# The second narrow self attention of a decoder, kept in float32 row bands with its projections and its end inside one loop, in place of split bf16 stacks through HBM

## The reference

```python
def layer_norm(x, w, b, eps=1e-05): ...
def attention(x, w_qkv, b_qkv, w_o, b_o):          # H = 16, dh = 8, B = 4, T = 512
    qkv = x @ w_qkv + b_qkv
    q, k, v = jnp.split(qkv, 3, axis=-1)           # each (B, T, 16, 8)
    scores = jnp.einsum('bqhd,bkhd->bhqk', q, k) / jnp.sqrt(jnp.float32(dh))
    probs = jax.nn.softmax(scores, axis=-1)
    ctx = jnp.einsum('bhqk,bkhd->bqhd', probs, v).reshape(B, T, D)
    return ctx @ w_o + b_o
h = x + attention(layer_norm(x, ln1_w, ln1_b), w_qkv, b_qkv, w_o, b_o)
return h + moe_ff(layer_norm(h, ln2_w, ln2_b), w_gate, w1, b1, w2, b2)
```

## Time and profile before

| | us |
|---|---|
| median of 3 runs (lowest, highest) | 2156.8 (2144.95, 2158.94) |
| the profiled execution: its time, its span | 2162.13, 2160.4 |
| from the end of stage b's last `XT` copy (565.7) to the end of stage c's (970.9) | 405.2 |
| TensorE, VectorE, ScalarE busy over the span | 1709.4, 1297.4, 1013.1 |
| mean granted TensorE clock over the span | 0.893 |

### The profile page before, as it was taken

The page is one execution under the profiler, slowest core; times in us unless marked ns, Lnnn a source line. Parts: engine busy times, 40 slices in busy tenths (PEclk is TensorE's granted clock), DMA queues, the critical chain, the costliest instruction groups (busy, mean ns, idle before and its releaser), DMA issues. The chain is left out here.

```text
span 2160.4 us, 32545 instructions
## 1 busy us (share of the span) xinstructions
PE 1709.4 (79%) x9889; PEld 969.6 (45%) x9942; DVE 1297.4 (60%) x4106; ACT 1013.1 (47%) x1938; POOL 153.7 (7%) x280
## 2 busy tenths in 40 slices
PE   4187877287416955969999499999999989989997
PEld 2044444154201321336777344454545455656664
DVE  7388896565735844733333487767676745764445
ACT  3188884075103633643334167667576643332221
POOL 2000000300100000010000100000000002330000
PEclk8599998598756987988999799999999998998999
DMA  1533400340152124001000110000000000000000
GB/s 56 81 40 40 44 0 3 57 56 8 41 81 31 20 26 44 1 3 40 20 20 10 39 40 1 1 1 1 1 1 1 1 1 3 1 1 23 22 15 27
DMA packets 57630, 48.74 MB, mean 23 GB/s; under 512 B 12692, under 2 KB 53048, under 8 KB 57528
## 3 DMA queue, kind: packets, MB, share of 16 engines
q1 hardware_dynamic: 57527, 47.45, 13.8%
HBM read 38.30 MB, written 8.91 MB: 22 GB/s over the span
## 5 line engine op out<-in xcount | busy, mean ns | idle before, releaser
L557 DVE TENSOR_REDUCE c_NM<-ps_t 128x1 f32<-128x512 f32 x256 | 169.9, 688 | 96.9 <-PE ps_t L437 95.2
L1556 ACT ACTIVATE d_PT<-ps_t 128x512 f32<-128x512 f32 x256 | 150.5, 589 | 105.8 <-PE ps_t L1472 105.8
L1547 ACT ACTIVATE d_PR<-d_PR,d_NM 128x512 f32<-128x512 f32 x256 | 183.9, 718 | 32.9 <-DVE d_NM L1618 32.9
L437 PE MATMUL ps_t<-KX,QX 96*128 (+1 forms) x256 | 108.3, 428 | 105.6 <-DVE c_IB L575 46.8
L619 ACT ACTIVATE c_PT<-ps_s 128x1024 f32<-128x1024 f32 x128 | 130.4, 1024 | 126.6 <-PE ps_s L460 124.5
L2358 DVE SCALAR_TENSOR_TENSOR X<-ps_t,GATE,X 128x128 f32<-128x128 f32 x272 | 76.6, 344 | 185.3 <-PE ps_t L2283 185.3
L762 ACT ACTIVATE a_PR<-a_PR,a_NM 128x128 f32<-128x128 f32 (+3 forms) x256 | 129.8, 555 | 78.8 <-DVE a_NM L743 78.8
L1618 DVE CUSTOM_DVE_ANT_0 d_PR<-ps_s,d_BH 128x512 f32<-128x512 f32 x256 | 165.4, 683 | 0.3 <-PE ps_s L1463 0.2
L672 PE MATMUL ps_t<-ident,a_PR 128*128 128x128 f32 x640 | 117.9, 295 | 49.8 <-ACT a_PT L686 37.4
L2320 ACT ACTIVATE f_HT<-ps_s,f_BE 128x512 f32<-128x512 f32 x128 | 87.9, 687 | 128.6 <-PE ps_s L2273 127.8
L1463 PE MATMUL ps_s<-d_K,d_Q 64*128 64x512 f32 x512 | 145.0, 644 | 1.3 <-DVE d_NM L1618 1.3
(11 more groups left out here) (330 smaller groups left out, 2989.8 us busy)
## 6 DMA issues: line engine op xcount, KB each, us to landing
QX<-split_parts SPq DMA_DIRECT2D x108, 128.0 KB
KX<-split_parts SPq DMA_DIRECT2D x72, 128.0 KB
f_W<-in_L_ffn_w SPq DMA_DIRECT2D x16, 256.0 KB, 3.1
split_parts<-a_PARTS SPq DMA_DIRECT2D x8, 384.0 KB, 10.3
split_parts<-c_PARTS SPq DMA_DIRECT2D x8, 384.0 KB, 10.6
g_W<-in_L_ffn_w SPq DMA_DIRECT2D x24, 128.0 KB, 2.3
split_parts<-b_PARTS SPq DMA_DIRECT2D x4, 384.0 KB, 10.7
X<-in_x SPq DMA_DIRECT2D x4, 256.0 KB
```

The lines of the kernel that those rows point to most:

```text
L437: nc.tensor.matmul(c.ps_t[:, i % 2, :], QX[0:SROWS, bass.ds(head, 1), qt * P:(qt + 1) * P], KX[0:SROWS, bass.ds(head, 1), :], start=True, ...
L557: nc.vector.tensor_reduce(NM[:, qt, j:j + 1], c.ps_t[:, i % 2, :], AX.X, ALU.max, negate=True).then_inc(maxed, 1)
L1547: nc.scalar.activation(PR[:, n % RING, e, :], PR[:, n % RING, e, :], ACT.Exp, scale=-1.0, bias=NM[:, n % RING, e:e + 1], accum_out=DEN[:, ...
L1556: nc.scalar.activation(PT[:, g % 2, e, :, qt * P:(qt + 1) * P], c.ps_t[:, e, :].rearrange("p (k q) -> p k q", q=P), ACT.Copy).then_inc(tak ...
```

## The change

Stage c no longer uses the stacks, the split or HBM. Queries and keys are projected group by group inside the loop, with weights padded so that head `j` of a group lies at partitions 32j to 32j+7 of `QG` and `KG` (float32). `score` multiplies 8 rows in float32, in the row group of its head (array tiles of 32 rows x 128 columns); row 32j+8 of `KG` is one (a bias) and row 32j+8 of `QG` gets the negated maxima, so `score_by_key` multiplies 9 rows. The maxima are turned once in float32 (16 x 128) and written by four DMAs a step. The names: `MBANKS`, two banks for the tiles whose maxima are taken; `KPAIRS`, two pairs of banks for the exponents; `ps_f`, the one bank that projections, turned maxima, turned heads and the output projection share in a fixed order (`shared_bank_free`). `score` runs 24 tiles ahead of `score_by_key`. Value products are 512 columns an instruction. The output projection, residual, norm and `XT` copy of a batch are spread over the steps of the next one. All 16 steps are written out, with no hardware loop. The weights are loaded by `finish` of stage b, ahead of its own (`early`). Stage b's block no longer sets rows 96 to 127 of `KX` to one. With it the stores and loads of `split_parts` for stage c, 8 and 72 DMAs, are gone.

```diff
+class NarrowWeights:
+    def __init__(self, c, tag, ctx):
+        self.W = c.sb(f"{tag}_W", [P, 3, P], F32, ctx)
+        self.WO = c.sb(f"{tag}_Wo", [P, P], F32, ctx)
+        self.BROW = c.sb(f"{tag}_Brow", [1, 3, P], F32, ctx)
+        self.BV = c.sb(f"{tag}_Bv", [P, P], F32, ctx)
+        self.BO = c.sb(f"{tag}_Bo", [P, P], F32, ctx)
+        self.WB = c.sb(f"{tag}_WB", [P, 2], F32, ctx)
+        self.loaded = c.sem(f"{tag}_w")
...
+    MAXIMA_LEAD = 24
+    ALL = STEPS * TILES
+    MBANKS = [c.ps_s[:, i, :] for i in range(2)]
+    KPAIRS = [c.ps_s[:, 2:4, :], c.ps_t[:, :, :]]
+    PTS = 3
...
+        QG = c.sb(f"{tag}_QG", [P, 3, S], F32, own)
+        KG = c.sb(f"{tag}_KG", [P, 3, S], F32, own)
+        VG = c.sb(f"{tag}_VG", [P, 2, QT, H, CW], F32, own)
+        NM = c.sb(f"{tag}_NM", [P, 2, GH, QT], F32, own)
+        NMT = c.sb(f"{tag}_NMT", [TILES, 2, P], F32, own)
+        PT = c.sb(f"{tag}_PT", [P, PTS, GH, S], F32, own)
...
+        def head(j, rows):
+            return slice(CW * j, CW * j + rows)
...
+                for u in range(STEPS):
+                    sp.wait_ge(s_nm, u + 1)
                     for j in range(GH):
+                        sp.dma_start(QG[CW * j + HD8:CW * j + HD8 + 1, u % 3, :].rearrange("a (k q) -> a k q", q=P),
+                                     NMT[j * QT:(j + 1) * QT, u % 2, :]).then_inc(s_row, 16)
+                sp.wait_ge(s_row, rows_all * STEPS)
...
+                nc.gpsimd.memset(WP[:, :, :, :], 0.0).then_inc(s_zero, 1)
+                nc.gpsimd.memset(BP[:, :, :, :], 0.0).then_inc(s_zero, 1)
+                nc.gpsimd.memset(ONE[:, :], 1.0).then_inc(s_zero, 1)
...
+                def queries(u):
+                    shared_bank_free(pe, ("q", u))
+                    nc.tensor.matmul(c.ps_f[:, :], padded(0, u % GROUPS), columns(u // GROUPS), start=True,
+                                     stop=True).then_inc(s_q, 1)
...
+                def score(m):
+                    u, i = divmod(m, TILES)
+                    qt, j = divmod(i, GH)
+                    if i == 0:
+                        pe.wait_ge(s_qout, u + 1)
+                        pe.wait_ge(s_kout, u + 1)
+                    if m >= 2:
+                        pe.wait_ge(s_max, m - 1)
+                    nc.tensor.matmul(MBANKS[m % 2], QG[head(j, HD8), u % 3, qt * P:(qt + 1) * P], KG[head(j, HD8), u % 3, :],
+                                     start=True, stop=True).then_inc(s_m, 1)
+                def turn_maxima(u):
+                    pe.wait_ge(s_max, TILES * (u + 1))
+                    shared_bank_free(pe, ("n", u))
+                    nc.tensor.transpose(c.ps_f[0:TILES, 0:P], NM[:, u % 2, :, :].rearrange("p h q -> p (h q)"),
+                                        c.ident[:, :]).then_inc(s_nt, 1)
+                def score_by_key(m):
+                    t, i = divmod(m, TILES)
+                    kt, j = divmod(i, GH)
+                    j = (j + 2) % GH
+                    if i == 0:
+                        pe.wait_ge(s_row, rows_all * (t + 1))
+                    if m % 2 == 0 and m >= 4:
+                        pe.wait_ge(s_exp, m // 2 - 1)
+                    nc.tensor.matmul(KPAIRS[m // 2 % 2][:, m % 2, :], KG[head(j, HD8 + 1), t % 3, kt * P:(kt + 1) * P],
+                                     QG[head(j, HD8 + 1), t % 3, :], start=True, stop=True).then_inc(s_st, 1)
+                def value_products(w):
+                    t, kt = divmod(w, QT)
+                    b, g = divmod(t, GROUPS)
+                    pe.wait_ge(s_exp, GH // 2 * (w + 1))
+                    if kt == 0:
+                        pe.wait_ge(s_vout, b + 1)
+                        if t:
+                            pe.wait_ge(s_ct, t)
                     for j in range(GH):
+                        mm = nc.tensor.matmul(c.ps_v[head(j, CW), :], VG[:, b % 2, kt, g * GH + j, :], PT[:, w % PTS, j, :],
+                                              start=(kt == 0), stop=(kt == QT - 1))
+                    mm.then_inc(s_pv, 1)
...
+                pe.wait_ge(s_zero, 4)
+                pe.wait_ge(s_pad, 4)
+                bias_columns()
+                queries(0)
+                keys(0)
+                values(0)
+                queries(1)
+                keys(1)
+                for m in range(MAXIMA_LEAD):
+                    score(m)
+                turn_maxima(0)
+                for m in range(ALL):
+                    t, i = divmod(m, TILES)
+                    b, g = divmod(t, GROUPS)
+                    if m + MAXIMA_LEAD < ALL:
+                        score(m + MAXIMA_LEAD)
+                    score_by_key(m)
+                    if i % GH == GH - 1 and m >= TILES // 2 - 1:
+                        w = m // GH - 1
+                        value_products(w)
+                    if i == 0 and t + 2 < STEPS:
+                        queries(t + 2)
+                    if i == 4 and t + 2 < STEPS:
+                        keys(t + 2)
+                    if i == 7 and t:
+                        turn_heads(t - 1)
+                    if i == 9 and t + 1 < STEPS:
+                        turn_maxima(t + 1)
+                    if i == 13:
+                        if g == 0 and b + 1 < B:
+                            values(b + 1)
+                        if g == 1 and b:
+                            turn_context(b - 1)
+                        if g == 2 and b:
+                            output(b - 1)
+                        if g == 3 and b:
+                            back(b - 1)
...
+                def exp(m):
+                    w, j = m // GH, (m % GH + 1) % GH
+                    act.wait_ge(s_st, m + 1)
+                    if j == 2 and w >= PTS:
+                        act.wait_ge(s_pv, w - PTS + 1)
+                    nc.scalar.activation(PT[:, w % PTS, j:j + 2, :], KPAIRS[m // 2 % 2], ACT.Exp).then_inc(s_exp, 1)
...
+                queries_out(0)
+                queries_out(1)
+                maxima_out(0)
+                for m in range(ALL):
+                    t, i = divmod(m, TILES)
+                    b, g = divmod(t, GROUPS)
+                    if m % 2:
+                        exp(m)
+                    if i == 1 and t + 2 < STEPS:
+                        queries_out(t + 2)
+                    if i == 5 and t:
+                        heads_out(t - 1)
+                    if i == 10 and t + 1 < STEPS:
+                        maxima_out(t + 1)
+                    if i == 14 and g == 1 and b:
+                        context_out(b - 1)
+                    if i == 14 and g == 3 and b:
+                        columns_out(b - 1)
...
+                def maximum(m):
+                    u, i = divmod(m, TILES)
+                    qt, j = divmod(i, GH)
+                    dve.wait_ge(s_m, m + 1)
+                    if i == 0 and u >= 2:
+                        dve.wait_ge(s_nt, u - 1)
+                    nc.vector.tensor_reduce(NM[:, u % 2, j, qt:qt + 1], MBANKS[m % 2], AX.X, ALU.max,
+                                            negate=True).then_inc(s_max, 1)
...
+                keys_out(0)
+                values_out(0)
+                keys_out(1)
+                for m in range(MAXIMA_LEAD):
+                    maximum(m)
+                for m in range(ALL):
+                    t, i = divmod(m, TILES)
+                    b, g = divmod(t, GROUPS)
+                    if m + MAXIMA_LEAD < ALL:
+                        maximum(m + MAXIMA_LEAD)
+                    if i == 5 and t + 2 < STEPS:
+                        keys_out(t + 2)
+                    if i == 8 and t:
+                        normalise(t - 1)
+                    if i == 14 and g == 0 and b + 1 < B:
+                        values_out(b + 1)
+                    if i == 14 and g == 2 and b:
+                        residual(b - 1)
+                    if i == 15 and g == 2 and b:
+                        statistics(b - 1)
+                    if i == 6 and g == 3 and b:
+                        apply(b - 1)
...
-        nc.gpsimd.memset(c.KX[SROWS:P, :, :], 1.0)
...
-            finish(c, "b", "ctx", wo=a["L0_xattn_Wo"], bias=a["L0_xattn_bo"], pre=(a["L0_ffn_ln1_w"], a["L0_ffn_ln1_b"]))
-            q, k, v = (slice(i * P, (i + 1) * P) for i in range(3))
-            w, b = a["L0_ffn_w_qkv"], a["L0_ffn_b_qkv"]
-            narrow_self_attention(c, "c", w[:, q], w[:, k], w[:, v], scratch, b[q], b[k], b[v], qscale=ISQ8)
-            finish(c, "c", "ctx", wo=a["L0_ffn_w_o"], bias=a["L0_ffn_b_o"], mode="inner",
-                   pre=(a["L0_ffn_ln2_w"], a["L0_ffn_ln2_b"]))
+        with ExitStack() as own:
+            weights = NarrowWeights(c, "c", own)
+            finish(c, "b", "ctx", wo=a["L0_xattn_Wo"], bias=a["L0_xattn_bo"], pre=(a["L0_ffn_ln1_w"], a["L0_ffn_ln1_b"]),
+                   early=lambda sp: weights.load(sp, *(a[f"L0_ffn_{n}"] for n in
+                                                       ("w_qkv", "b_qkv", "w_o", "b_o", "ln2_w", "ln2_b"))))
```

(33 more changed lines are left out.)

417 lines of the change are left out of this document (224 added, 193 removed).

## The result

The changed kernel takes 2391.2 us (median of 4 runs, 2387.4 to 2391.4), the kernel before 2156.1 (4 runs, 2145.0 to 2158.9): a ratio of 1.110, 95% interval 1.106 to 1.114. It is 235 us slower where 107 less were forecast. The profiled execution took 2391.2.

The account below looks back on a forecast made before the run. No engine bounds stage c as a whole; 112 us are DMA waits. Terms 3.2 + 4.5 + 9 + 21 + 5 + 233 + 22 = 298 us against 405, 107 saved: 2050 us, 8-in-10 range 2022 to 2112.

Parts of the forecast that it names:

- the price of a score: Stage c's float32 scores: one 512-column matmul lasts 0.59 us warm and holds the array 0.43.
- the four of L1463: Stage d matmuls on 64 rows, taken as two overlapping pairs, 1.13 us in all; cited against rivals A and C.
- the round: Stage c, one maxima bank through score, reduction and hand-overs: 1.48 us; two banks give a tile per 0.74, sixteen 11.8.
- a block: Stage c, 512 columns of other TensorE work between scores: takes 0.66 us and stretches the step by 0.46.
- the slack of 0.20 a slot: Stage c, TensorE held 0.54 us of each 0.74 slot; other work stretches slots only by what exceeds the remaining 0.20.
- rival B: Clock stays at half through stage c, from bank waits or 8 busy rows: 2164 us, no change; chance 0.08.
- The lead: Start of stage c: 24 scores ahead with nothing beside them, 18 us warm, 24 cold, 21 taken.
- the entry: Start of stage c: clears, weight padding and bias products 4.5 us, first projections through one shared bank 9.
- the register rows: TensorE rows that vanish with the change, inside the old 14.1 us step and costed at nothing.
- Rival A: Row groups in stage c don't overlap: step 19.4 us, +56, total 2106; chance 0.11.
- C: Slower rival: every change of row group drains the array, step 25.7 us, +150, total 2200; chance 0.06.
- (5): Rival theory of the follow-up experiments: something else in the new stage, such as the row DMAs, costs; no size or chance.

Follow-up runs that it names:

- e2: Changed kernel with scores and scores by key contracting all 128 rows, without overlap of row groups (output not the reference's): 2344.3 us, 1.084 of the kernel before.
- e4: Changed kernel with one more bfloat16 matmul of 128 rows and 512 columns ahead of each score: 2656.1 us, 1.229 of the kernel before.
- e1: Changed kernel with scores and scores by key on all 32 rows of their row group, added rows zero: 2167.4 us, 1.003 of the kernel before.
- e5: Changed kernel with bfloat16 queries, keys and maxima row, and all 32 rows of each group: 2073.6 us, 0.960 of the kernel before.
- e6: Kernel before with the KX memset cut into 16 pieces and moved into stage b's attention: 2149.2 us, 0.995 of the kernel before.
- e3: Changed kernel with bfloat16 queries, keys and maxima row, still 8 and 9 rows: 2101.4 us, 0.972 of the kernel before.
- e9: Bfloat16 queries, keys and maxima on 32 rows, with exponents and values bfloat16 too, against the kernel before: 2082.4 us, 0.966.
- e8: Changed kernel with the KX memset put back in stage b: 2403.2 us, 1.113 of the kernel before.

## Why the prediction was wrong

**Two steps failed. The first** is the price of a score: "eight in a row took 3.60, so one holds the array (3.60 - 0.59)/7 = 0.43 us". The eight are records, and two records are one float32 matmul; the four of L1463 are two matmuls as well. The earlier trace rows has it in sight: x256 records of a line that has 128 matmuls (8 experts, 4 batches, 4 chunks), and so has the count here, 512 records to 256 reductions. A float32 matmul of 512 columns holds its rows for 0.86 us (e2), not 0.43. The Trainium skill (FP8 and Floating Point Precision, TensorE Precision Notes) says that true float32 takes four passes through the array. The trace has two records a matmul, and e4's agrees with four in time: at 1.2 GHz its float32 scores hold the array for 2.01 us (804.79 to 806.80) and its bfloat16 filler for 0.54 (804.25 to 804.79), a ratio of 3.7. With the right count the round is 1.90 instead of 1.48 and a block 1.02 instead of 0.66; and the slack of 0.20 a slot, credited against each block, isn't there. The step becomes 22.3 (e1), 6.6 more than 15.7, and 14 steps are 92 us: nearly the whole 107. e1 gives no change, e5 gives the 15.7 back.

**The second, and the larger, is the clock,** which the sum takes as full: the condition of rival B came true, at a wrong price. The clock stayed at half "because the waits for banks, or arrays with 8 busy rows of 128, leave the engine too idle". Of its two reasons e1 leaves the rows. The forecast held 0.91 in stage a against it; in that trace the matmuls of 120 to 200 all use 128 rows, which says nothing of 8. B was priced with the same halved matmul, a step of 22.8 and 2164; it is 37.7 and 2391. Against the kernel before, the clock is 224 of the 235 us lost (2391.2 less e1's 2167.4, one run), and the price of a score is what would have been the gain. The forecast had a rival for the clock and none for the price of a float32 matmul, so none for both together.

**The lead and the entry.** 24 scores took 575.8 to 610.2, 34.4 us for the 21 forecast (24 x 2.86/2 = 34.3: the same two errors). From 550.3 to the first score 25.5 passed, for 4.5 + 9: the five projections go through the shared bank at 2.9 us each instead of 2.0 (13.7 in all instead of 9), the bias products and their copy take 3.7 instead of 1.3, and VectorE's copies of weights cost 6.0 instead of 1.2, again beside GpSimd:

```profile
552.51 3.50 POOL L533 MEMSET c_VG<- 128x4096 f32 x1
...
552.69 3.47 DVE L822 COPY c_WP<-c_W 128x128 f32<-128x128 f32 x2 [4.37 <-POOL c_BP L532]
```

**Costed at nothing.** The row DMAs are hidden, as forecast: the only waits of scores by key for `c_QG` in the steps are one of 3.6 us for a weight load and one of 2.0 for a matmul, both ahead of the first step. The removed memset was not free to begin with: "ran while its block waited for DMA" doesn't hold, since the cast that it held up stands ahead of the stores that the block waits for. It gave 9 us back. No run prices the register rows. Stage a ended 6 us earlier than before in this trace; it did so, by 5 to 8, in every later profile, that of e6 too, so that belongs to the one execution of before and is no effect of the change.

**What was right.** DMA stalls of 112 us are gone. The seven early loads cost 9.20 - 5.38 = 3.8 of wait for 3.2 forecast. Rival A falls (starts 0.02 apart), and C as well: in e1 the changes between scores and scores by key cost nothing that the sum lacks. What is left of (5) is the entry.

The parts of the miss, profile against profile: 14 periods of 36.8 instead of 15.7 and a last one of 30.1 instead of 13.4, 312 us; lead 13; entry 12; tail 1196.9 - 1159.7 = 37 instead of 22, 15 (counted from 4.0 behind the last turned maxima, where the first scores by key stand; 10 of it is the clock, since from those maxima to the end e1 takes 31.6 and this kernel 41.2); first rows 1 less; behind the stage 3; ahead of it 19 less (memset 9, stage a 6, and 4 that stage b was shorter beyond that, which is within its scatter: it takes 170.1 to 177.6 from profile to profile without the memset). Together 335, and the profiled time is 2391.2 - (2162.1 - 107) = 336 above the forecast.

## What to carry to other kernels

Count records against instructions before a duration is divided by a count: the number of a group's records beside that of the reductions or copies that consume it shows how many passes a matmul takes in that type. Ask of a stream of matmuls how much of the array it fills at a time: padding 8 rows with zeros to 32, in four row groups, took 224 us from this kernel and cost nothing, and did nothing where two scores ran at a time (e1's lead). A GpSimd memset over SBUF belongs beside work of VectorE that reads PSUM (e6, 10 us less).

## What the runs showed of the hardware

- A float32 matmul is two records, each with a weight load; on 512 columns 1.12 us from start to end at 2.4 GHz (e1) and 2.08 at 1.2 GHz. At 2.4 GHz it holds the array 0.86 us (e2).
- The granted clock was 0.50 for 640 us with TensorE busy 91 of 100 us on 8 and 9 rows, and 0.97 with it busy 88 on 32 rows of zeros and data (e1). By the Trainium skill (TensorE: Matmul & The Clock Gate, What's actually happening) the clock goes by how busy the engine has been. The busy time of these profiles does not bear that out: the busier of these two streams has the lower clock, and in float32 the rows made the difference. Scores with 32 rows, at most two at a time, were at 0.50 (e1's lead), with 128 rows at 0.90 (e2's); a 128-row matmul ahead of each 8-row score left it at 0.53 (e4).
- With bfloat16 scores the clock went up and down from step to step (0.52 to 1.00 in e5), with 8 rows too (0.79 in e3). Less work for TensorE came with a lower clock (0.55 in e9) and no shorter time; why is open.
- A VectorE cast of 0.43 us took 9.4 (kernel before) and 9.6 (e8) beside a GpSimd memset of 13.75, and 0.43 in the profiles of the changed kernel and of e6, where it isn't.
